# Attention normalised along features instead of along tokens: the denominators and their reciprocals go through DRAM

## The reference

```python
qkv = x @ Wqkv
q, k, v = jnp.split(qkv, 3, axis=-1)          # 16 heads of 16
logits = jnp.einsum('bihd,bjhd->bhij', q, k) * scale
logits = logits + SLOPES[None, :, None, None] * rel[None, None, :, :]
logits = jnp.where(causal[None, None, :, :], logits, -jnp.inf)
attn = jax.nn.softmax(logits, axis=-1)
out = jnp.einsum('bhij,bjhd->bihd', attn, v).reshape(Bc, Tc, Dc)
x = _layernorm(x + out @ Wout)
h = jax.nn.silu(x @ wg.T) * (x @ wu.T)         # 768 wide, weights / 127
x = _layernorm(x + h @ wd.T)
```

## Time and profile before

| what | us |
|---|---|
| median of three runs | 2136.79 |
| profiled execution | 2136.29 |
| its span, first to last instruction | 2134.6 |
| PE busy, share of the span | 1983.0, 93% |
| DVE busy | 1595.1, 75% |
| ACT busy | 1223.5, 57% |
| POOL busy | 928.5, 43% |
| DMA queue 1 | 226 MB, 48.5% of 16 engines |

### The profile page before, as it was taken

The page is one execution under the profiler, slowest core; times in us unless marked ns, Lnnn a source line. Parts: engine busy times, 40 slices in busy tenths (PEclk is TensorE's granted clock), DMA queues, the critical chain, the costliest instruction groups (busy, mean ns, idle before and its releaser), DMA issues.

```text
span 2134.6 us, 47883 instructions
## 1 busy us (share of the span) xinstructions
PE 1983.0 (93%) x19236; PEld 1550.0 (73%) x19236; DVE 1595.1 (75%) x2765; ACT 1223.5 (57%) x1999; POOL 928.5 (43%) x1924
## 2 busy tenths in 40 slices
PE   4779999999999999999999999999999999999986
PEld 3557777777777777777777777777877877777766
DVE  4557777787777787777778777778777778777754
ACT  1446656555655656655655665565565665566552
POOL 0123444444444453444454444444344445444444
PEclk8789999999999999999999999999999999999998
DMA  7455455355555445545545545545554544553500
GB/s 205 103 120 105 101 112 118 96 112 114 115 112 110 103 108 106 128 103 108 113 100 112 121 109 111 116 97 114 106 122 109 106 109 102 111 125 91 100 16 21
DMA packets 148830, 229.09 MB, mean 107 GB/s; under 512 B 13552, under 2 KB 64496, under 8 KB 148592
## 3 DMA queue, kind: packets, MB, share of 16 engines
q1 hardware_dynamic: 148608, 226.02, 48.5%
HBM read 139.98 MB, written 84.93 MB: 105 GB/s over the span
## 4 chain that ended last, share of the span: by engine, by line
PE 80%; DVE 10%; ACT 5%; DMA 2%; issue 1%; SPq 1%; POOL 0%; POOLq 0%; DVEq 0%
PE pair L495 72%; PE pair L498 8%; DVE row_max L801 7%; ACT probs L726 3%; DVE staged_lo L786 2%; ACT staged_hi L704 2%; DMA q_rows<-max_lo 1%; SPq L471 0%; DMA q_rows<-bounce 0%; DMA probs<-L_attn_Wout 0%; SPq L480 0%; DMA bounce<-staged_lo 0%; DVE row_max L803 0%; DVE xt_lo L786 0%; DVE x1t_lo L786 0%
## 5 line engine op out<-in xcount | busy, mean ns | idle before, releaser
L726 ACT ACTIVATE probs<-pair 128x1024 f32<-128x1024 f32 x640 | 627.1, 1027 | 150.1 <-PE pair L495 149.8
L903 POOL TENSOR_SCALAR_AFFINE_SELECT probs<-probs 128x256 f32<-128x256 f32 (+1 forms) x896 | 371.5, 440 | 445.9 <-ACT probs L726 445.1
L910 POOL TENSOR_TENSOR h_lo<-h_full,h_hi 128x256 fp32r<-128x256 f32 x384 | 283.2, 738 | 507.6 <-ACT h_hi L751 496.9
L803 DVE TENSOR_REDUCE row_max<-pair 128x8 f32<-128x1024 f32 x256 | 312.6, 1221 | 115.2 <-PE pair L495 114.7
L801 DVE TENSOR_REDUCE row_max<-pair 128x2 f32<-128x1024 f32 x256 | 311.9, 1218 | 71.2 <-PE pair L495 71.2
L495 PE MATMUL pair<-q_rows,k_rows 64*128 64x512 f32 (+3 forms) x2048 | 321.0, 370 | 38.4 <-DMA q_rows<-max_lo 20.8
L495 PE MATMUL pair<-k_rows,q_rows 52*128 52x512 f32 (+3 forms) x2048 | 299.6, 351 | 60.2 <-DVE staged_lo L786 26.1
L495 PE MATMUL pair<-probs,v_ones 128*32 128x512 f32 (+3 forms) x4096 | 319.3, 441 | 0.8 <-ACT probs L726 0.8
L495 PEld LDWEIGHTS pair<-q_rows,k_rows 64*128 64x128 f32 x2048 | 167.8, 188 | 157.2 <-ACT probs L726 92.2
L495 PEld LDWEIGHTS pair<-k_rows,q_rows 52*128 52x128 f32 x2048 | 179.0, 190 | 122.9 <-DVE row_max L801 62.9
L704 ACT ACTIVATE staged_hi<-pair 128x512 fp32r<-128x512 f32 x128 | 76.6, 599 | 269.9 <-PE pair L495 260.5
(11 more groups left out here) (88 smaller groups left out, 3622.7 us busy)
## 6 DMA issues: line engine op xcount, KB each, us to landing
bounce<-staged_hi SPq DMA_DIRECT2D x128, 256.0 KB
bounce<-staged_lo SPq DMA_DIRECT2D x128, 256.0 KB
q_rows<-bounce SPq DMA_DIRECT2D x128, 256.0 KB, 5.2
k_rows<-bounce SPq DMA_DIRECT2D x128, 256.0 KB, 6.2
x_sb<-L_attn_x SPq DMA_DIRECT2D x32, 512.0 KB, 10.4
k_rows<-bounce SPq DMA_DIRECT2D x128, 128.0 KB, 5.5
q_rows<-bounce SPq DMA_DIRECT2D x128, 128.0 KB, 6.7
x<-L_attn_x SPq DMA_DIRECT2D x32, 512.0 KB, 9.1
```

Of the source, the lines that this page charges most:

```text
L726: scalar.activation(probs[g][:, tile, :, :], pair[:, :, :], ACT.Exp, scale=scale).then_inc(s_exp, 1)
L803: vector.tensor_reduce(maxima[:, QB2_PARTS:QB0 + 1, :, p].rearrange("p b s -> p s b"), pair[:, :, :].rearrange("p s (b n) -> p s b n", n=P ...
L903: made = pool.affine_select(out=diagonal, in_=diagonal, compare_op=ALU.is_ge, fill=0.0, base=0, pattern=[[0, diagonal.shape[1]], [1, P]], ...
L910: pool.tensor_tensor(h_lo[:, m, :], h_full[(n_split_h[step] - 1) % H_BUFFERS][:, :], h_hi[:, m, :].bitcast(F32), ALU.subtract).then_inc(s_ ...
```

## The change

The weighted sums stay with features on partitions. The steps `turn` and `transposed("attn")` go. In their place, for each unit u and group g:

- `send`: SP stores the 128x512 tile of sums and denominators to DRAM (`pv_bounce`).
- `fetch`: SP waits until that has landed, then loads the 64 feature rows into `attn` (two units' buffers, 128 partitions by 512 tokens) and, in a second DMA, the 4x512 denominators spread over 128 partitions by 16 (`sums`).
- `recip`: DVE takes the 128x16 reciprocals.
- `send_recip`: SP stores them to DRAM; `fetch_recip`: SP waits until that has landed, then loads them with each head's row repeated over its 16 partitions (`recips`).
- `divide`: one 128x512 product per unit on DVE; `attn_hi` on ACT and `attn_lo` on POOL split it for `out`.

For group 1 of unit w-2, `send` and `fetch` follow `pv_copy` in the middle of `attention(w)`, and `recip`, `send_recip` and `fetch_recip` end it. For group 0 of unit w-1, `send` is in `attention(w)`, `fetch` opens `rest(w)`, and the reciprocals follow the fifth feed-forward tile. `rest` is put in another order too: `divide` after feed-forward tile 1, `max_row` after tile 2, both `out` steps after tile 5.

```diff
                     self.add("pv_copy", u, g)
+                    self.add("send", u, g)
+                    if g == 1:
+                        self.add("fetch", u, g)
...
         self.norms()
+        self.reciprocal(w - 2, 1)
         if self.has(w):
             self.add("combine", w)
...
+    def reciprocal(self, u, g):
         if self.has(u):
-            self.take("turn", u, g)
-            self.add("divide", u, g)
+            self.add("recip", u, g)
+            self.add("send_recip", u, g)
+            self.add("fetch_recip", u, g)
...
+        if self.has(w - 1):
+            self.add("fetch", w - 1, 0)
         if self.has(w + 1):
             self.add("gather", w + 1)
...
+        if has_ffn:
+            self.gate_up(ffn, part, range(0, 2))
+        self.divide(w - 2)
+        if has_ffn:
+            self.gate_up(ffn, part, range(2, 3))
+        self.max_row(w)
+        self.split_attn(w - 2)
+        if has_ffn:
+            self.gate_up(ffn, part, range(3, 5))
+        self.reciprocal(w - 1, 0)
...
+                elif kind == "fetch":
+                    e.wait_ge(s_sent[z][g], (u // 2 + 1) * 16)
...
+                    sync.dma_start(attn[z][g * HALF:(g + 1) * HALF, :], pv_bounce[z, g, :, 0, :, :]).then_inc(s_fetched[z][g], 16)
+                    sync.dma_start(sums[z][:, g, :],
+                                   pv_bounce[z, g, :, 1, 0, :].rearrange("h (a n) -> h a n", n=sums[z].shape[2])).then_inc(s_fetched[z][g], 16)
+                elif kind == "send_recip":
+                    e.wait_ge(s_recip, n_recip["recip", u, g])
...
+                elif kind == "fetch_recip":
+                    e.wait_ge(s_recip_sent[z][g], (u // 2 + 1) * 16)
...
+                    sync.dma_start(recips[z][g * HALF:(g + 1) * HALF, :], wide).then_inc(s_recip_fetched[z][g], 16)
...
+                elif kind == "divide":
+                    vector.tensor_tensor(attn[z][:, :], attn[z][:, :], recips[z][:, :], ALU.mult).then_inc(s_divide, 1)
```

More of the change, by code:

```diff
@@ L168, in project, with values, divide, split_attn @@
                 self.add("spread", u)
[L170 to L175, removed]
-        if self.has(u):
-            self.take("turn", u, g)
-            self.add("divide", u, g)
+    def values(self, b, t0):
+        self.take("values", b, t0)
+        self.add("values_out", b, t0)
+    def reciprocal(self, u, g):
+        if self.has(u):
+            self.add("recip", u, g)
+            self.add("send_recip", u, g)
+            self.add("fetch_recip", u, g)
+    def divide(self, u):
+        if self.has(u):
+            self.add("divide", u)
+    def split_attn(self, u):
+        if self.has(u):
+            self.add("attn_hi", u)
+            self.add("attn_lo", u)
     def max_row(self, u):
@@ L221, in rest @@
                     self.add("load_x", k + 2)
[L222 to L226, removed]
-            self.project(w + 2, 0)
[L228 to L236, removed]
+        else:
+            self.project(w + 2, 0)
             if w == -1:
                 self.ffn_weights()
[L239 to L255, removed]
+        if has_ffn:
[8 more added lines that the diff above has]
+        self.reciprocal(w - 1, 0)
+        if has_ffn:
+            self.gate_up(ffn, part, range(5, 6))
+        if part == 0:
+            self.project(w + 2, 0)
+        if has_done:
+            self.project_out(done, 0)
+            self.project_out(done, 2)
+        if has_ffn:
+            self.down(ffn, part)
+        if has_done:
+            self.add("norm1", done, 0)
+            self.norms_due.append(("norm1", done, 2))
+        self.project(w + 2, 1)
     def ffn_weights(self):
@@ L295, in build @@
     order = plan.order
-    n_work = tally(order, "x", "attn", "x1", "project", "values", "max_row", "turn", "out", "gate_up", "down", "weight")
+    n_work = tally(order, "x", "x1", "project", "values", "max_row", "out", "gate_up", "down", "weight")
     n_first, n_row_max, n_combine = tally(order, "first"), tally(order, "row_max"), tally(order, "combine")
@@ L629, in _ @@
                     made.then_inc(s_pv, 1)
[L631 to L637, removed]
                 elif kind == "out":
@@ L732, in _ @@
                     if u >= 1:
-                        e.wait_ge(s_work, n_work["turn", u - 1, g])
+                        e.wait_ge(s_sent[(u - 1) % 2][g], ((u - 1) // 2 + 1) * 16)
                     scalar.activation(pv_t[g][:, :], bank, ACT.Copy).then_inc(s_pv_copy, 1)
+                elif kind == "attn_hi":
+                    u, = key
+                    e.wait_ge(s_divide, n_divide["divide", u])
+                    if u >= 2:
+                        e.wait_ge(s_work, n_work["out", u // 2 - 1, 2])
+                    scalar.activation(attn_hi[:, u % 2, :], attn[u % 2][:, :], ACT.Copy).then_inc(s_attn_hi, 1)
                 elif kind == "tanh":
```

97 lines of the change are left out of this document (62 added, 35 removed).

## The result

The changed kernel takes 2650.36 us, the median of four runs (2633.91 to 2657.74), against 2136.52 us beside it: 1.2395 times the time before, interval 1.2335 to 1.2455. That is slower, as forecast, but 300 us over the 2350 us of the forecast and beyond its range.

A forecast was written before the change was run, and what follows sets the result against it. PE's work bounds the kernel before; after, SP's chain ahead of the gather. Pair 2 x 20.8 + 28.2 = 69.8 us against 63.23, +195 us over 29.5 batches, plus 11 and 5 on 2136.3: 2350 us, range 2200 to 2450.

The forecast's parts named there:

- steps 1 to 4: SP's chain from window start through denominators, reciprocal, its store and load issues: gather begins at 20.8 us instead of 14.6.
- step 2: Reciprocal on DVE stands behind the ten reductions, starting 16.2 us into the window and done at 16.45.
- Step 3: `send_recip`: 0.1 us of semaphore plus an 8 KB landing in DRAM, taken as 2.2 us (bounds 1.84 and 3.9).
- step 5: First gather DMA to PE's start: 12.7 us in an odd rest, 16.1 in an even one, 28.2 for a pair.
- the sum: Whole-kernel total: 2136.3 + 195 steady state + 11 first two windows + 5 at the end, say 2350 us.
- the prediction's own sign: In the changed profile, gather starting at 21 us but a window far over 37 us would point to the quarter of the engines.
- the third rival: Loads ahead of gather use 4 of 16 DMA engines, landing 0.8 to 4.2 us later per window; up to 2600 us; chance 9%.
- PE's 84 us: 24 transposes per batch leave PE, all on the path: 2.62 us x 32 batches = 84 us.
- The second rival: PE's wait moves to `out`, odd window ending after `divide` and `attn_lo`: 21 us less, 2115 us; chance 3%.
- The first: Rival: SP's chain fits into the slack before the gather is needed, transposes are pure gain: 2052 us; chance 4%.

The follow-up runs named there:

- no_land: `plain_all` without SP's two waits for a landing (of the stores of sums and of reciprocals), output wrong: 2250.78 us, 1.0544 of before.
- plain_all: Changed kernel with the `attn`, `recips` and denominator loads all reading contiguous rows of x over all engines, wrong data: 2334.8 us, 1.0933 of before.
- plain_both: Changed kernel with the `attn` and `recips` loads reading 64 contiguous rows of x, spread over 16 engines, wrong data: 2341.79 us, 1.0967 of before.
- no_trips: Changed kernel without the normalisation's four transfers and their waits, DVE multiplying constants, output wrong: 2092.91 us, 0.9796 of before.
- merged: `merged_late` with the two loads of x back in their old place, between gather and `store_max`: 2448.37 us, 1.1457 of before.
- merged_late: Changed kernel with one fetch and reciprocal round trip per unit, 16-row reciprocals, earlier `recip`, x loads behind `store_max`: 2375.78 us, 1.1114 of before.

## Why the prediction was right and wrong

**Right: the bound and the direction.** SP's chain in front of the gather is what sets each window, PE waits for the store of the maxima in every one, and the mean granted clock falls with it, from 0.981 to 0.881.

**Right: steps 1 to 4.** Gather was to start 20.8 us in and started 20.2 us in by the mean (19.5 and 20.0 in the windows shown). The reciprocal was where step 2 had it: it starts 16.1 and 16.6 us in (1227.51 and 1268.71 on DVE's timeline), and `send_recip` follows at 16.3 and 16.8, against 16.45. Step 3 took `out`'s 2.2 us for a landing of 8 KB; it is 1.39 us, below even the lower bound of 1.84. `no_land`, without the waits for this landing and for that of `send`, is 84 us faster than `plain_all`.

**Wrong: step 5, "from the first gather DMA to PE's start".** It took 28.2 us for a pair from the kernel before, where no load stands right ahead of the gather; the loads on a quarter of the engines were put at nothing there. Here 256 KB on few engines stood ahead of it, and the measured way is 38.8 us, 10.6 us more. The gather itself starts 1.3 us a pair earlier than forecast, which gives a little back: 79.19 - 69.8 = 9.4 us, times 29.5 pairs 277 us of the 300 us of the miss. The rest lies in the fill and the tail, which lost 43 us where the sum had 16. With the loads spread (`plain_both`) the way is 29.2 us, close to the fill's own 28.8, and the time is 8 us from the forecast. It is also the prediction's own sign: the gather at its place, and the windows (41.6 us for an even one) far over 37 us.

This was the third rival. Its mechanism was read rightly from the outer sizes and the share of 0.50, its price was not: between 0.8 and 4.2 us a window the argument leaned to the small one and gave the large one's 2600 us a chance of 9%. Measured is (38.8 - 29.2)/2 = 4.8 us. By the Trainium skill, "DMA: Bandwidth & Descriptors", section "Rules for kernel authors", an outermost dimension below 16 confines a DMA to at most as many engines; the trace agrees, by the 5 updates against 16, the packets and the 0.27 of the share.

The large price came near the measured one, but its rate per engine is not shown. In the middle of `attention` the `attn` load takes 4.3 us on 4 engines and 2.9 us on 16. That is 1.4 us for 24 KB more on each engine, an estimate of 18 GB/s, much nearer to the stores' 22.8 than to the gather's 10.4. Only with the gather right behind it does the load take 8.3 us. So what was mis-sized is the load together with the gather on the same few engines. The sentence against the rival (the gather's rate is set by its few partitions) had no row, and no run settles it.

**Half right: PE's 84 us.** They were taken as wholly on the path. In `no_trips` 44 us of them come back. In the sum this did not show, since there the wait swallows PE's saving. It shows in the waits: `plain_both`, which has nearly the forecast's windows, waits 1.9 and 3.4 us by the mean instead of 3.8 and 5.4. How much of this is the transposes and how much the lower clock (0.929) was not separated.

**The second rival** was present in small: PE waits 47.8 us for `attn_lo`, in odd rests. By the order of the steps this comes behind the store of the maxima, so it should only shorten the wait for the gather; no run takes it out. **The first** was far off: even without landings and few engines the kernel is 5.4% slower (`no_land`).

**Small errors.** The product was priced at 0.69 us and takes 0.82, `attn_lo` at up to 1.5 and takes 1.28. The loads of x stood in step 5 only as the 3.4 us between its even and its odd way; `merged` against `merged_late` gives 3.0 us a pair where the gather is exposed.

## What to carry to other kernels

Before a DMA is put in front of another on one queue, look at its outer size, and price what it holds up on the few engines that it uses, not by the mean share of all sixteen. A price read where no gather follows the load (1.4 us here) is too low: with 1.5 MB behind, two such loads cost 4.8 us a window. Where a transfer has only a few us of slack, count each wait, issue and load that is put in front of it, the harmless ones too. Work taken off the bounding engine returns only where nothing hid behind it: some of the transposes had covered a chain through ACT and DVE.

## What the runs showed of the hardware

- DMAs of 128 KB with 4 as outer size use about 4 of 16 engines: 5 semaphore updates against 16, 12 packets fewer for each, and shares of 0.57, 0.27 and 0.14 in the last 3 us of the even window shown. The number of semaphore updates in the trace goes with the outer size: 5 for 4, 9 for 8, 16 for 16 and more.
- Two of them ahead of 1.5 MB lengthen the way from gather to PE by 4.8 us a window. All four of a unit spread over 16 engines bring 308 us.
- The same 128 KB load on 4 engines takes 4.3 us with no gather behind it and 8.3 us with the gather behind it; on 16 engines it takes 2.9 us in both places.
- The effects of the two kinds of load don't add up: 190 and 33 us alone, 308 together.
- The landing of a 256 KB store: median 2.1 us in the changed kernel, 4.3 us in `merged_late`, where 1 MB of `spread` is queued just ahead (4.2 us in the window shown). It is 1.39 us for 8 KB in a quiet queue.
- A wait of PE has an echo: the slice after 7.94 us of wait runs at a granted clock of 0.50 (1.2 GHz), where the steady state before was at 1.00.
